# Rotary-attention stage of a fused block: GpSimd's operations regrouped between VectorE's subtractions

## The reference, cut to what matters

```python
q = _apply_rope(proj(Wq, bq))      # x1*cos - x2*sin and x2*cos + x1*sin
k = _apply_rope(proj(Wk, bk))
v = proj(Wv, bv)
...
# blocks of 128 queries see their own block of keys and the one before it
scores = jnp.einsum('bhnqd,bhnkd->bhnqk', qb, kcat) * scale
...
scores = jnp.where(valid[None, None], scores, jnp.asarray(-1e+30, scores.dtype))
attn = jax.nn.softmax(scores, axis=-1)
ctx = jnp.einsum('bhnqk,bhnkd->bhnqd', attn, vcat)
...
return merged @ Wo.T + bo
```

## Time and profile before

| | |
|---|---|
| median of the runs | 1590.65 us |
| the profiled execution | 1588.3 us, its span 1586.5 us |
| TensorE busy | 1496.7 us, 94% of the span |
| VectorE busy | 1408.8 us, 89% |
| ScalarE busy | 1323.4 us, 83% |
| GpSimd busy | 1109.6 us, 70% |
| granted TensorE clock, mean | 0.983 |

### The profile page before, as it was taken

How to read it: one execution, slowest core, us unless ns; L and a number is a source line. 1 busy time by engine, 2 the same in 40 slices (tenths; PEclk the granted TensorE clock), 3 DMA queues, 4 the chain that set the end, 5 groups by cost and what they waited for, 6 DMA issues and landing times.

```text
span 1586.5 us, 46990 instructions
## 1 busy us (share of the span) xinstructions
PE 1496.7 (94%) x16866; PEld 1145.7 (72%) x16866; DVE 1408.8 (89%) x3875; ACT 1323.4 (83%) x2442; POOL 1109.6 (70%) x894
## 2 busy tenths in 40 slices
PE   5999978899999999999999999999999999889998
PEld 4888745577777677777777777776777777678887
DVE  5998769999999999999999999999999999857885
ACT  5999758888888888888888888888888888759996
POOL 4665367777787887877787877877787777634443
PEclk7999999999999999999999999999999999989999
DMA  6232347999999999999999999999999998862331
GB/s 216 94 114 91 99 84 141 163 172 179 179 183 175 176 167 184 172 184 181 173 179 169 175 182 181 176 179 175 171 170 172 174 165 162 165 163 87 107 107 67
DMA packets 729886, 247.94 MB, mean 156 GB/s; under 512 B 689588, under 2 KB 716472, under 8 KB 729656
## 3 DMA queue, kind: packets, MB, share of 16 engines
q1 hardware_dynamic: 711816, 228.93, 76.3%
q10 hardware_dynamic: 17840, 16.00, 3.7%
HBM read 47.73 MB, written 25.17 MB: 46 GB/s over the span
## 4 chain that ended last, share of the span: by engine, by line
PE 73%; ACT 8%; DVE 7%; issue 6%; DMA 4%; SPq 1%; POOL 1%; POOLq 0%; DVEq 0%; ACTq 0%
PE banks L1675 19%; PE banks L1790 14%; PE banks L1762 6%; PE banks L1692 6%; PE banks L730 6%; PE banks L698 6%; PE banks L712 5%; DVE at_prob L1341 3%; PE banks L1746 3%; ACT at_prob L1514 3%; DMA at_pt<-at_halves 3%; PE banks L1748 3%; PE banks L1747 3%; PE banks L683 2%; ACT at_v_h L1532 1%
## 5 line engine op out<-in xcount | busy, mean ns | idle before, releaser
L1514 ACT ACTIVATE at_prob<-at_prob,at_top 128x256 f32<-128x256 f32 (+1 forms) x1024 | 428.4, 490 | 21.4 <-DVE at_top L1341 19.7
L1341 DVE CUSTOM_DVE_ANT_0 at_prob<-banks,at_masks,pre_s_scale 128x256 f32<-128x256 f32 (+1 forms) x1024 | 421.2, 471 | 22.0 <-PE banks L1790 4.7
L1353 DVE TENSOR_TENSOR at_halves<-at_prob,at_halves 128x1024 f16<-128x1024 f32 (+1 forms) x256 | 330.9, 1293 | 4.8 <-ACT at_halves L1523 4.8
L1675 PE MATMUL banks<-at_xt,pre_w_h 128*128 128x512 f16 x1024 | 297.4, 383 | 8.8 <-ACT at_v_l L1542 5.8
L1790 PE MATMUL banks<-at_kt,at_qt 32*128 32x256 f32 (+1 forms) x4096 | 252.9, 383 | 33.3 <-issue 26.0
L1523 ACT ACTIVATE at_halves<-at_prob 128x1024 f16<-128x1024 f32 (+1 forms) x256 | 263.3, 1029 | 6.1
L1790 PEld LDWEIGHTS banks<-at_kt,at_qt 32*128 32x128 f32 x4096 | 198.4, 187 | 94.6 <-issue 90.1
L1240 POOL TENSOR_TENSOR at_qt<-at_q_by 128x512 f32<-128x512 f32 x128 | 222.2, 1755 | 0.0
L1746 PE MATMUL banks<-at_v_h,at_pt 128*128 128x65 f16 x1984 | 209.3, 196 | 9.9 <-DMA at_pt<-at_halves 6.0
L1220 POOL TENSOR_TENSOR at_q_by<-at_q_first,at_tables 128x512 f32<-128x512 f32 x128 | 163.2, 1276 | 76.1 <-DVE at_halves L1353 73.9
L1746 PEld LDWEIGHTS banks<-at_v_h,at_pt 128*128 128x128 f16 x1984 | 182.7, 98 | 44.4 <-issue 25.5
(11 more groups left out here) (125 smaller groups left out, 3320.4 us busy)
## 6 DMA issues: line engine op xcount, KB each, us to landing
f_x<-in_x SPq DMA_DIRECT2D x16, 512.0 KB, 3.7
x_after_ffn<-f_x SPq DMA_DIRECT2D x16, 512.0 KB, 2.6
f_x<-x_after_attention SPq DMA_DIRECT2D x16, 512.0 KB, 4.4
out_x<-f_x SPq DMA_DIRECT2D x16, 512.0 KB, 3.0
at_x_res<-x_after_ffn ACTq DMA_DIRECT2D x61, 128.0 KB, 2.6
x_after_attention<-at_x_res ACTq DMA_DIRECT2D x58, 128.0 KB, 2.0
at_x_ln<-x_after_ffn SPq DMA_DIRECT2D x32, 128.0 KB, 2.9
at_tables<-in_cos SPq DMA_DIRECT2D x16, 256.0 KB, 3.5
```

Source lines behind the costliest of these rows:

```text
L1341: last = nc.vector.tensor_tensor_reduce(out=prob[:, n % 2, h, low:2 * P], in0=s_ps[:, h, n % 2 * 2 * P + low:(n % 2 + 1) * 2 * P], in1=mas ...
L1353: nc.vector.tensor_tensor(parts[:, 1, :, :], prob[:, n % 2, :, keys_from(t, b):2 * P], parts[:, 0, :, :], ALU.subtract).then_inc(p_low, 1)
L1514: last = nc.scalar.activation(at, at, ACT.Exp, bias=top[:, n % 2, h:h + 1], scale=-1.0)
L1675: last = nc.tensor.matmul(pr_ps[:, half, :].rearrange("p (b t) -> p b t", b=SB), w[wp][:, k, at:at + P], xt[:, r, :, xp, k, :], start=n == ...
```

## The change

In GpSimd's `at_step(t)` three things change. The row low half `x_low_of(t + 7)` goes from the front of the list to behind `bias_rows`. The sum `key(t + 1, 1)` goes ahead of the wait for sub0. The second query product goes ahead of the wait for sub1, and the last sum, `query(t + 1, 0)`, gets a wait for sub2 ahead of it. On ScalarE, `carry_keys` is issued at the end of the step that it belongs to and no longer in the middle of the next.

```diff
@@ gpsimd, at_step(t)
             after_p_low(t - 1, 3)
-            if t + 7 >= SB:
-                x_low_of(t + 7)
             context_low(t - 2)
             key_product(t + 1, 0)
             key_product(t + 1, 3)
+            key(t + 1, 1)
             after_p_low(t, 0)
-            key(t + 1, 1)
             query_product(t + 1, 0)
+            query_product(t + 1, 3)
             after_p_low(t, 1)
-            query_product(t + 1, 3)
             key(t + 1, 0)
             query(t + 1, 1)
+            after_p_low(t, 2)
             query(t + 1, 0)
             bias_rows(t - 4)
+            if t + 7 >= SB:
+                x_low_of(t + 7)
             if g == 3 and S >= -2:
                 inverse_std(S + 3)
@@ scalar, at_step(t)
             query_copy(t + 1)
-            carry_keys(t - 1)
             exponentials(t, 1)
...
                 x_high_of(t + 8)
+            carry_keys(t)
             key_copy(t + 2)
```

## The result

The changed kernel took 1614.19 us, the median of three runs (1612.88 to 1616.47), against 1590.65. The medians differ by 23.5 us. The ratio on record is 1.0158 with a 95% interval of 1.0144 to 1.0172, so the change is slower. The forecast was 1624 us, slower. The profiled execution took 1616.5 us with a span of 1614.7, 28.2 more than the profiled one of before.

A forecast was written before the change was run, and what follows sets the result against it. A slackless 18.42 us ring through GpSimd, VectorE, ScalarE and TensorE was taken as the bound. Sixteen steps sum to 303.7 us, +0.56 a step; 60 x 0.56 = 33.6 on 1590.65 gives 1624 us, range 1588 to 1640.

The forecast's parts named there:

- the ring: Whole step, sub3's end to the next, through GpSimd, VectorE, ScalarE and TensorE: 10.12 + 8.30 = 18.42 us, no slack.
- step with a short sub0: One step in four, sub0 of 512 elements: it arrives before the key sum; 8.30 + 9.96 = 18.26 us a step.
- The ring closes without remainder: The whole step's pieces add up to 18.42 us, used as evidence against hidden slack.
- rivals 1 and 2: 1: faster, scores gate decides, 1564 or 1577, chance 0.14; 2: no change, ScalarE makes up, 1590 to 1593, chance 0.06.
- The gate at the scores: TensorE's 0.45 us wait for GpSimd's last query sum goes, but a wait at the keys replaces it: worth nothing.
- both rings: The sub3-to-sub3 ring and a second through last query sum and scores: same length, 18.42 us, both bind.
- The dependence on the own engine: GpSimd's key sum directly follows the product it reads: 0.12 us more ahead of sub1, net +0.73.
- The 0.28 us for the shift: VectorE's shift inside a query sum, once in four steps: VectorE 0.28 us later behind the keys, 3 x 0.28.
- One sign named in advance: GpSimd's wait ahead of its first operation in the step shrinks from 1.67 us.
- The same in either order: Ahead of sub1: if sub0 slipped in before the key sum, sub1 would be as late; the work's sum counts.
- Rival 3: Sub3 meets GpSimd's inverse deviation: GpSimd's next list begins 0.95 us later in 13 steps, +12, 1636 us; chance 0.15.

The follow-up runs named there:

- s3: Changed kernel, DMAs copying without turning, with the first key sum alone put back behind the wait for sub0: 1582.7 us.
- w1: Changed kernel, DMAs copying without turning, with each step's last four exponentials on 128 of 256 columns: 1597.8 us.
- u1: Changed kernel, DMAs copying without turning, with the two key products in the other order: 1606.3 us.
- s2: Kernel before, DMAs copying without turning, with only the first key sum ahead of the wait for sub0 and carried keys at the step's end: 1582.5 us.
- u2: Kernel before, no turning; row low half last, second query product before sub1's wait in long-sub0 steps, both query sums behind a sub2 wait: 1585.7 us.
- s4: Kernel before, DMAs copying without turning, with the row low half alone moved behind the bias row: 1582.4 us.
- s1: Changed kernel, DMAs copying without turning, with the row low half back in front of GpSimd's list: 1608.5 us.
- r0: Kernel before, with DMAs copying without turning and scores scaled to nearly nothing, compute instructions all kept: 1581.9 us.

## Why the prediction was right, and where it was not

**The direction and the ring: right.** The prediction split the step into 10.12 us from sub3 to sub1 and 8.30 us behind it, and gave 10.85 + 8.30 = 19.15 for the change. Measured: 10.82 to 10.84, and 19.14. The step with a short sub0 was given as 18.26; most take 18.21. Each half is shown by a run of its own: s3 takes the key sum out of the front and the whole loss goes; w1 takes 0.41 us from ScalarE behind sub1 and each plain step falls by 0.43.

**"The ring closes without remainder": no evidence.** The prediction used this against rivals 1 and 2. But it found the keys' start of the step before by taking 18.42 off the next one (711.94), so its pieces had to add up to 18.42, with slack or without. What shows that there is no slack is that the second part stays put when the first one moves: 8.30 us behind sub1's end where sub1 ends at 10.07 and 10.11 (before), 9.98 (s3), 10.66 (u1), 10.83 (after) and 9.91 (its short steps). Where sub1 was not held up itself (1.22), it is 8.42 (s2: 9.94 and 18.36).

**The gate at the scores: right.** It went, and was worth nothing, since the wait for the low half of the values took its place. That both rings bind is right too, within 0.05 us: in the kernel before, plain ordinary steps take 18.38 where sub1 ends at 10.07, and 18.42 where sub0 waits longer for the queries behind the scores (it comes at 5.22, and sub1 ends at 10.11). u2 and s4 show that the gate is real where sub1 comes early.

**The dependence on the own engine: right in kind, too small.** I took 0.12. The gap of 0.13 is what shows in the trace; with the overlap of neighbours u1 gives 0.17. Without it sub1 ends at 10.66, where the sum had 10.12 + 0.61 = 10.73: the rest was 0.07 too large, most of it because the 10.12 holds a wait of sub0 for the queries that the change removes (10.07 without it). The two misses nearly cancel, and that 10.85 met 10.83 so closely is luck to this extent.

**The sum: 33.6 us against 23.5 (medians) or 28.2 (the two profiled executions).** Over the 57 steps of the table it is 30.6 us where 0.56 x 57 = 31.9 was forecast. The rest is outside them (3.1 us ahead after five steps, four of which I had set to nothing), and in which executions were profiled: that of before lies 2.35 us below its median, that of after 2.3 above.

**The small operations of the layer norm: one term too wide, one missed.** The 0.28 us for the shift shows by itself in 3 of the 12 steps of the table that have it, as 0.25. The prediction did not see another operation of 128x4 on VectorE, the variance (`at_veps`), once in four steps. Alone it takes 0.17 us (at 198.54 in the trace of before). Before the change it started inside the last query sum, and the key products behind it came 0.19 us late; after, it meets the shorter bias row and they are on time. VectorE before, and after:

```profile
731.19 1.00 DVE L1387 TENSOR_SCALAR at_veps<-at_mv 128x4 f32<-128x4 f32 x1
```

```profile
740.56 0.68 DVE L1388 TENSOR_SCALAR at_veps<-at_mv 128x4 f32<-128x4 f32 x1
```

The steps with it took 18.60 before against 18.41 for their neighbours, and 19.14 after like all others. So the change gives 0.19 back in one ordinary step of four, and this is part of why the mean gain in the table is 0.63 and not 0.73.

**One sign named in advance did not come.** GpSimd's wait ahead of its first operation was to shrink from 1.67; it grew to 2.05. The prediction's own pieces say so: the list behind sub2 ends 2.7 us later, and sub3 ends 3.4 + 1.21 behind sub2. The other signs came: sub0 of 2.14, the wait for the low half of the values (0.7 us in 35 steps), 1.17 ahead of the first query product, steps of 19.14 and 18.21.

**"The same in either order": wrong.** To the doubt that sub0 might slip in first, the prediction answered that the amount of work ahead of sub1 counts. s2 and s1 refute this. GpSimd's list does not hold VectorE up; only the one operation that is running when a subtraction arrives does. If sub0 goes first, the key sum and all behind it move back, sub1 arrives 2.3 us behind sub0's end and goes in ahead of the next operation. The loss hangs on 0.21 us (key sum at 4.80, sub0 at 5.01), not on 0.61 us of work. The forecast came out because the sum does start first in the ordinary steps, as its main line said; for sub0 slipping in first, the prediction would have given the same 1624 us, and been wrong.

**Rival 3: its mechanism came, at another price.** The inverse deviation takes 2.10 us and not 1.02 in 12 of its 13 times in the attention stage: it is sent at 742.59, sub3 arrives at 742.60, and it is the deviation that stands still. GpSimd begins its next list 0.78 us late, where 0.95 was said. But that moves the key sum behind sub0, so sub0 only meets the products (1.52 us, as in this row), and what follows is the race at sub1. VectorE in two such steps, 742 to 756 us and 586 to 602 us, sub0 and sub1 of each:

```profile
748.84 1.52 DVE L1354 TENSOR_TENSOR at_halves<-at_prob,at_halves 128x1024 f16<-128x1024 f32 x1
...
752.68 1.22 DVE L1354 TENSOR_TENSOR at_halves<-at_prob,at_halves 128x1024 f16<-128x1024 f32 x1
```

```profile
594.57 1.52 DVE L1354 TENSOR_TENSOR at_halves<-at_prob,at_halves 128x1024 f16<-128x1024 f32 x1
...
598.41 2.37 DVE L1354 TENSOR_TENSOR at_halves<-at_prob,at_halves 128x1024 f16<-128x1024 f32 x1
```

Six of nine were won (sub1's end 10.08, in four of them a step of 18.5), three lost (11.24, steps of 19.54 to 19.80). I had priced +0.95 a step; the mean of these steps is 0.06 below the other ordinary ones.

**Rivals 1 and 2** did not come. Rival 2's idle time of VectorE ahead of the key products is still there (12.3 us in 19 steps), as it must be when ScalarE is in the ring.

**Still open.** Why the deviation wins against sub3 when it is sent 0.2 us earlier and seems to lose at 0.01. The boundary is narrow: started 0.09 us ahead of sub3 (1173.93 and 1174.02 in the trace of before; 0.10 ahead in s2) it still takes 1.02. The recorded starts don't tell who asked first. Nor was it tried to move the deviation out of sub3's way.

## What to carry to other kernels

When two engines lock each other out, count from the common event to the moment at which each is sent, not the work between: a subtraction pays for the one operation that runs when it arrives, and 0.2 us of order is worth 1 us. Put a long operation either behind a wait for the other engine or late enough to come second for certain; two arrivals within 0.02 us are a coin that the kernel throws in every step. And before moving work on an engine with 70% load, follow the ring through all engines, and test it for slack with steps of different lengths in the same trace: a part that stays the same behind an earlier and a later event has none. A sum that closes because one of its pieces was taken as the rest proves nothing. Where two rings are close to each other, a hold-up in one of them can cost nothing (sub3 in u2 and s4); the steps in which it is missing show it.

## What the runs showed of the hardware

- An elementwise operation of GpSimd with SBUF inputs and a VectorE subtraction with two SBUF inputs go in turn. A subtraction that had to wait ended 1.08 us behind the GpSimd operation (730.76 and 731.84); a GpSimd sum of 1.27 us took 2.09 when it was sent 0.13 us behind the products that VectorE already waited for (s2). In the trace this shows as a longer instruction and not as a wait.
- In a race within 0.02 us either can win (s1: 21 to 10). The four runs of s1 scatter over 16 us, the five of s2, with a wait in that place, over 1.9. That the races make the scatter is argued and not shown: the six runs of r0 scatter over 7.1.
- A small GpSimd operation (128x4, 1.02 us) can run beside a subtraction that starts 0.20 or 0.09 us later, and takes 2.10 us when both start within 0.01 us, at no cost for the subtraction (1.21).
- A small VectorE operation (128x4, 0.17 us alone) that starts inside a GpSimd operation ends with it: 1.00 us, until 732.19, where the query sum ends at 732.16.
- ScalarE, TensorE and VectorE behind sub1 took 8.30 us in steps from 18.2 to 19.1 us long, where sub1 had been held up.
- The Trainium skill (SBUF — State Buffer, Who interferes with whom) states that issue order, not the shape of the operation, decides who blocks. The large operations agree: key sum at 4.80 and subtraction at 5.01 gives 2.14 us for the subtraction; subtraction ahead of the sum gives 1.29, and 2.09 for the sum. The 128x4 deviation does not: issued 0.09 us first, it blocks nobody.
